# The second attention step with three score buffers, tiles prepared two ahead, and the unit matrix of R added as rows by GpSimd

## What is computed

```python
R = S + eye(N); R = R / R.sum(-1)            # S is adj here, N = 4096
Xf = Xa = X
for n in range(2):                           # two steps
    logits = (Xa @ W1.T @ W2.T) @ (Xa @ W3.T).T
    probs = softmax(logits)                  # 4096 x 4096
    A = the largest entries of each row up to a mass of 0.9, renormalised
    Xf = R @ Xf
    Xa = A @ Xa
    Z = Z + Xf @ U1[n].T + Xa @ U2[n].T
out = layernorm(X + Z) * ln_g + ln_b
```

## Time and profile before

| | |
|---|---|
| median of 3 runs | 4354.27 us (4349.45 to 4354.54) |
| the profiled execution | 4350.77 us |
| its span, first to last instruction | 4349.0 us |
| PE busy in the span | 3762.5 us (87%) |
| DVE busy | 3623.6 us (83%) |
| ACT busy | 3114.5 us (72%) |
| GpSimd busy | 1017.3 us (23%) |

### The profile page before, as it was taken

One profiled execution on the slowest core, in us unless ns is written; L12 is line 12 of the kernel. 1 busy time (PEld: TensorE's weight loads), 2 busy tenths in 40 slices (PEclk: granted clock), 3 DMA queues, 4 the chain that ended last, 5 costly groups with the idle time before them and its releaser, 6 DMA issues.

```text
span 4349.0 us, 66313 instructions
## 1 busy us (share of the span) xinstructions
PE 3762.5 (87%) x25364; PEld 3163.1 (73%) x25364; DVE 3623.6 (83%) x6400; ACT 3114.5 (72%) x3128; POOL 1017.3 (23%) x1412
## 2 busy tenths in 40 slices
PE   8677877777777769999999749999999999999996
PEld 5677777777777747777778547777777777778875
DVE  2899999999999939888888188888888889999995
ACT  3789889898989845555555367777777777777771
POOL 0000000000000000001010224444444445555555
PEclk9899999999999989999999979999999999999998
DMA  3211111111111020000000212222233423333332
GB/s 116 93 45 66 45 55 56 47 64 47 64 47 64 27 78 12 19 16 19 16 17 17 87 35 85 87 83 88 88 93 93 134 90 105 107 107 105 100 104 73
DMA packets 131759, 292.49 MB, mean 67 GB/s; under 512 B 14122, under 2 KB 94186, under 8 KB 127058
## 3 DMA queue, kind: packets, MB, share of 16 engines
q1 hardware_dynamic: 131410, 287.99, 20.6%
HBM read 250.19 MB, written 37.75 MB: 66 GB/s over the span
## 4 chain that ended last, share of the span: by engine, by line
PE 34%; ACT 28%; DVE 14%; issue 14%; POOL 10%; DMA 1%; DVEq 0%; SPq 0%; ACTq 0%; POOLq 0%
PE ps L803 11%; PE ps L642 9%; DVE b L1226 7%; ACT b L871 6%; ACT b L988 5%; ACT b L989 5%; DVE b L1173 3%; ACT b L865 3%; PE ps L792 3%; ACT b L971 3%; PE ps L748 3%; PE ps L623 2%; POOL b L468 2%; ACT b L859 1%; PE ps L780 1%
## 5 line engine op out<-in xcount | busy, mean ns | idle before, releaser
L707 PE MATMUL ps<-b 128*128 128x257 f32 x4096 | 902.1, 379 | 0.0
L803 PE MATMUL ps<-b 128*128 128x257 f32 x4096 | 900.9, 379 | 0.0
L642 PE MATMUL ps<-cb,b 128*128 128x128 f32 x4096 | 606.9, 312 | 321.7 <-ACT b L865 321.7
L707 PEld LDWEIGHTS ps<-b 128*128 128x128 f32 x4096 | 775.6, 189 | 118.3 <-issue 3.8
L803 PEld LDWEIGHTS ps<-b 128*128 128x128 f32 x4096 | 770.2, 189 | 111.7
L642 PEld LDWEIGHTS ps<-cb,b 128*128 128x128 f32 x4096 | 546.1, 163 | 371.1 <-ACT b L865 329.6
L1137 DVE SCALAR_TENSOR_TENSOR b<-b 128x4096 f32<-128x4096 f32 x128 | 566.4, 4425 | 63.1 <-ACT b L859 59.8
L1139 DVE CUSTOM_DVE_ANT_0 b<-b 128x4096 f32<-128x4096 f32 x128 | 566.3, 4425 | 5.5 <-DMA b<-in_adj 1.1
L871 ACT ACTIVATE b<-ps 128x1024 f32<-128x1024 f32 x512 | 499.9, 1023 | 75.6 <-PE ps L642 74.0
L623 PE MATMUL ps<-b 128*64 128x128 f32 x8192 | 504.0, 276 | 0.0
L865 ACT ACTIVATE b<-b 128x4096 f32<-128x4096 f32 x128 | 474.4, 3706 | 8.0 <-DVE b L1141 8.0
(11 more groups left out here) (186 smaller groups left out, 4743.2 us busy)
## 6 DMA issues: line engine op xcount, KB each, us to landing
b<-in_adjTb SPq DMA_DIRECT2D x256, 512.0 KB, 3.8
b<-in_adj SPq DMA_DIRECT2D x32, 2048.0 KB, 8.0
y_d<-b SPq DMA_DIRECT2D x64, 128.0 KB, 1.7
h_d<-b SPq DMA_DIRECT2D x64, 128.0 KB, 1.8
b<-h_d SPq DMA_DIRECT2D x64, 128.0 KB, 2.3
b<-in_xT SPq DMA_DIRECT2D x1, 4096.0 KB, 15.8
b<-in_x SPq DMA_DIRECT2D x32, 128.0 KB, 2.2
b<-y_d SPq DMA_DIRECT2D x32, 128.0 KB, 2.1
```

The source lines that it names most:

```text
L642: last = nc.tensor.transpose(bank(2 * (gq % 3), 2)[:, b * 128:(b + 1) * 128], ub[:, u % UB, j * 128:(j + 1) * 128], ident_s)
L707: last = mm(b[:, 0:XA], aj[:, q % AJR, e, :], xf[:, j, :], start=False, stop=(j == NT - 1))
L803: last = mm(o[:, 0:XA], at[:, q % ATR, b, :], xa[:, j, :], start=(j == 0), stop=(j == NT - 1))
```

## The change

In the second step there are three score buffers instead of two (`scores(s, t)` is `eb[:, t % 3]`, and the sums `zE` have three columns), and the tile that is prepared is two ahead: PE does `logits(n+2)` in iteration n, ACT copies it, exponentiates it only at the end of its iteration (`expo(n+2)` is the last call of `acts`), and GpSimd brackets it after `levels(n)`. `av_ev` and `mq_ev` move from ahead of the levels to behind level 1. DVE calls `rmax(t+2)` in `finish(t)`, between `mark` and the wait for the vote. Before the loop, tile 1's scores are made and exponentiated too. The first step keeps its order.

The unit matrix of R is no longer a product: `Rstart` only takes the PSUM bank, and `r_post` begins with one addition of 128 x 257 elements by GpSimd (`prs += xf[r]`).

To make room, AJR falls from 4 to 3, ACT's unused output `junk` is written as 8-bit floats instead of bf16, `gxs` shares `hin`, `u2` is loaded for one step at a time, `finx` has four buffers instead of six (SP waits for `f1` before it overwrites one), and the score buffers lose eight spare columns.

```diff
-    AJR = 4
+    AJR = 3
...
+        def scores(s, t):
+            return eb[:, t % (2 + s), 0:N]
...
+                    if m >= 2:
+                        sp.wait_ge(g["f1"], 2 * (m - 1))
...
                         po.wait_ge(g["rd"], r + 1)
+                        plink(tt(prs[:, i, :], prs[:, i, :], xf[:, r % NT, :], ALU.add))
...
                 if s == 1:
                     bracket(0)
+                    bracket(1)
...
                             r_post(p)
-                        if n + 1 < NT:
-                            bracket(n + 1)
...
                             levels(n)
+                        if n + 2 < NT:
+                            bracket(n + 2)
...
                 def Rstart(r):
-                    b = rslot()
-                    if r >= NT:
-                        pe.wait_ge(s_xl[r % NT // CT], 48)
-                    mm(b[:, 0:XA], ident_s, xf[:, r % NT, :], start=True, stop=False)
-                    return b
+                    return rslot()
...
-                    if n + 1 < NT:
-                        logits(n + 1)
+                    if n + 1 + s < NT:
+                        logits(n + 1 + s)
...
-                def acts(t, items):
+                def acts(t, items, n):
                     items = list(items)
                     for k in range(1, ACT_LEVELS + 1):
                         if t < NT:
                             level(t, k)
+                        if k == 1:
+                            if 1 <= n <= NT:
+                                av_ev(n - 1)
+                            if n >= 2 or n + 3 < NT:
+                                mq_ev(n - 2 if n >= 2 else None, n + 3 if n + 3 < NT else None)
                         if k >= ACT_LEVELS - 1 and items:
                             r_ev(items.pop(0))
                     for r in items:
                         r_ev(r)
+                    if n + 2 < NT:
+                        expo(n + 2)
...
                         for k in range(ACT_LEVELS + 1 if t else 1, r + 1):
-                            if k == r and t + 1 < NT:
-                                rmax(t + 1)
+                            if t == 0 and k == 3:
+                                rmax(1)
...
                     if s == 1:
                         mark(link, t, 0)
+                        if t + 2 < NT:
+                            rmax(t + 2)
```

More of the change, by code:

```diff
@@ L706, in Rpart @@
                             pe.wait_ge(s_xl[j // CT], 48)
-                        last = mm(b[:, 0:XA], aj[:, q % AJR, e, :], xf[:, j, :], start=False, stop=(j == NT - 1))
+                        last = mm(b[:, 0:XA], aj[:, q % AJR, e, :], xf[:, j, :], start=(j == 0), stop=(j == NT - 1))
                         if e == TBK - 1:
@@ L769, in mq @@
                         if tz is not None:
-                            last = mm(b[:, 0:256], xz[:, k, :], u2[:, s, k, :], start=(k == 0), stop=(k == 1))
+                            last = mm(b[:, 0:256], xz[:, k, :], u2[:, k, :], start=(k == 0), stop=(k == 1))
                     for k in range(2):
@@ L812, in _ @@
                 if s == 1:
+                    pe.wait_ge(s_l1, 16 * 10)
+                    mq(None, 2, zx(None, 2))
+                    logits(1)
                     Rmul(1)
@@ L1041, in _ @@
                 if s == 1:
+                    zx_ev(None, 2)
+                    mq_ev(None, 2)
+                    logit_ev(1)
+                    expo(1)
                     r_ev(1)
@@ L1057, in _ @@
                         zx_ev(tz, tx)
-                    if n + 1 < NT:
+                    if s == 0 and n + 1 < NT:
                         expo(n + 1)
-                    if 1 <= n <= NT:
-                        av_ev(n - 1)
-                    if zm:
-                        mq_ev(tz, tx)
-                    if s == 0 and tx is not None:
-                        gx_ev(tx)
-                    if s == 1:
-                        acts(n + 1, [2 * p + i for p in pairs_in(n) for i in range(2)])
+                    if s == 0:
+                        if 1 <= n <= NT:
+                            av_ev(n - 1)
+                        if zm:
+                            mq_ev(tz, tx)
+                        if tx is not None:
+                            gx_ev(tx)
+                    else:
+                        acts(n + 1, [2 * p + i for p in pairs_in(n) for i in range(2)], n)
                 barrier(ac, kS[s])
```

93 lines of the change are left out of this document (50 added, 43 removed).

## The result

The change makes the kernel slower: 4415.86 us in the median (4412.37 to 4417.04) against 4354.02 us (4349.45 to 4354.54) of the kernel before beside it, a ratio of 1.0143 with a 95% interval of 1.0125 to 1.0161. Forecast were 4374 us, between 4325 and 4400. The sign was right, the size was not.

The account below looks back on a forecast made before the run. It took PE's own round as the new bound, replacing a loop over four engines. Start +0.5, 28 rounds +26.6, ends -4.6, -5.2, -1.6, reload +7, on 4350.8, gave 4373.5, said as 4374 us, range 4325 to 4400.

Parts of the forecast that it names:

- T to E: Second step, end of second R product (T) to ACT's first `Tr` copy (E): 5.56 us each round, against 4.65 before.
- the stop behind the third chunk: PE's idle stretch after transposing three `Tr` chunks, waiting for a PSUM slot from ACT: 4.0 us each round.
- S to T: Start of `AV` (S) to the end of the next second R product: 43.2 us, from 44.08 less 0.88.
- the reload: Reload of xf at iteration 16, behind GpSimd's last R tiles: once +7 us, between 0 and 15.
- ring and 8-bit output: Three adj chunk buffers, if SP issues at once, and ACT's 8-bit `junk`: both to cost nothing on the path.
- E to S: ACT's first `Tr` copy to the start of `AV`: 8.5 us, depending on PE's clock, bounds 6.29 and 9.17.
- What is late next: PE's own round is late, `expo` standing before the first `Tr` copy: 57.3 us per round, +26.6 us over 28.
- The first rival: Clock holds or falls less behind PE's stop: 55.05 us per round and 4311 us if held; 4308 to 4345, chance 0.15.
- GpSimd drags SP: Rival: from iteration 17 late `r_post` delays SP's adj chunks, PE stops inside R products; +32, 4406 us, chance 0.12.
- It is still ready in time: DVE's mask, some 12 us early in the first half, about 10 us later in the second, never delays PE.
- The identity product: Removing R's identity products saves PE 0.88 us per round; GpSimd's addition, some 3 us per iteration, off the path.
- The third rival: PE goes free of ACT: T to E stays at its old mean of 4.65 us or shrinks; 4331 us, chance 0.10.

Follow-up runs that it names:

- the best version: Changed kernel with `expo` before the second R copy, `final_add` before the bracket, reload swap, one adj chunk before output stores, identity products back: 4251.21 us, ratio 0.977.

## Why the prediction was right or wrong

**What held.** The chain left DVE's search and went onto PE's round. `expo` starts 0.6 us after T, T to E is 5.53 to 5.55 us in nearly every round (5.56 said), the stop behind the third chunk 3.99 us (4.0 said), S to T 43.2 us. In the first half masks come some 12 us ahead of T, as said. The last iteration is 46.32 us (46.4 said), the reload +5.3 us over a round (+7 said), and ring and 8-bit output cost nothing: a pass of a level takes 3709 ns (L1000), as the 3.7 us of before.

**E to S, under "What is late next": mis-sized.** I took 8.5 us, from four rounds of before whose stop was like the new one. Over iterations 1 to 17 it is 153.92 / 17 = 9.05 us, with the clock at 0.63 in nearly all. One of the rounds and the sum, which answer to the earlier trace rows:

```profile
2786.24:2795.45 9.21, 8.14 (x28) 4.32 (x29) 8.99 (x9) 7.16 (x8) 8.93 (x7) 0.63 0.00 0
...
sum 153.92, PE 135.63 PEld 71.66 DVE 147.54 ACT 121.17 POOL 148.73; mean PE 7.98 PEld 4.22 DVE 8.68 ACT 7.13 POOL 8.75
```

The round settles at 58.00 us, and E to S then stays at 9.1 to 9.3 us, while before it went from 6.29 to 9.17. The four rounds of before with a like stop were no measure of it; even the upper bound of 9.17 was a little low. That the stop alone doesn't fix the price is shown by the run with the identity products: the same stop of 4.0 us, round after round, and 7.9 to 8.7 us behind it. In the first half the term comes to 14 x 0.55 = 7.7 of the 8.4 us. In the second E to S is 8.6 us in the mean, near the forecast. The first rival (the clock holds) is ruled out by the same rows, and its 55.05 us per round was right for the case in which it does hold: the run with eight filling products had 55.07.

**"GpSimd drags SP", the second rival: it was not an alternative but came on top.** I treated it as a case of 0.12 beside the forecast, though nothing in the forecast excluded it, and so the sum has nothing for PE's waits inside the R products. The step that failed is the position of `r_post`: I said the first chunk's issue at T + 34, from R tiles done by T + 28 or so. In the round shown they are done at T + 31.5, and the issue is at T + 38.2; over iterations 17 to 28 the R tiles are done between T + 27.6 and T + 31.5, and the issue is between T + 33.5 and T + 38.2. I had named one held instruction of the bracket, the row of 4.31 us. There are three in the round shown: two in the bracket (4.49 and 4.56 us) and one in `r_post` (4.73 us for the scaling), beside three passes of DVE. The need was nearly where I had it, T + 40.6 against T + 39.8. Here the rule that I called a smaller matter decides: the Trainium skill, SBUF — State Buffer, section Who interferes with whom, has such a GpSimd instruction wait while DVE's two-input pass holds the port. The rows fit it: the scaling takes 4.73 us beside L1255, a pass with two inputs, and ends with it, and 0.48 us one tile later beside L1261, which has one input. No run here took DVE's passes away. I had asked only whether DVE is held, not whether GpSimd is, and what waits behind it on SP's queue. The price of the lateness is paid twice here too. In the round shown above PE waits 1.95 us for the chunk, and then the other 80 instructions take 19.34 us; at the pace of the 48 ahead of the stop, 10.60 / 48 = 0.221 us each, they would take 17.7. The two make 3.6 us, and this round is 61.85 us where its neighbours without a stop have 57.9. Over 13 rounds it is 16.2 us of waits and 10.9 us of slower products, 27.1 of the 28.4 us. Iteration 30, which I had put at 52.1 us with no such stop at all, takes 61.54 us:

```profile
4264.25 15.95 PE L810 MATMUL ps<-b 128*128 128x257 f32 x64
...
4296.61 20.38 PE L714 MATMUL ps<-b 128*128 128x257 f32 x80 [5.11 <-DMA b<-in_adjTb]
```

It has the longest wait for a chunk, 5.11 us, and both `AV` (14.08 us at full clock) and the instructions behind the wait run at a low clock, 0.88 and 0.86 in the mean.

**"It is still ready in time", under "Three buffers, two tiles ahead": true, with nothing to spare.** From iteration 18 on the masks come between 3.5 us ahead of T and 0.5 us behind it, about the 12 less 10 us that I had said, and PE waits for them for 1.5 us in all, where I had said never. What I had not seen is where the 10 us come from: DVE waits for `final_add` for 62.5 us in 13 rounds, because that now stands behind the bracket. The run that moved only SP's loads gained about 10 us and then met the mask: 38.9 us of PE's waiting. So two things had almost no slack, and I had named only one of them as a rival.

**"The identity product": -0.88 us per round, forecast as a gain on the path, was none.** The run with the products put back had the same first half and, in its trace, a second half that was 11 us shorter. What I put "nothing on the path" for, GpSimd's addition, is on the path in the second half, by way of SP's queue. In the best version, where the two kernels ran side by side, the whole trade is 17 us the wrong way.

**The third rival** is ruled out, for the reason given: PE's slot is missing because ACT is late. I had weighed the Trainium skill, Perfetto Trace Analysis, section Optimization Strategy, by which a gap that repeats can mean too few buffers. The third score buffer left the stop and made it longer (3.99 us against 3.23 in the earlier trace rows); moving one call on ACT removed it. But with that call moved the change as a whole does pay, 51.6 us per round against 56.5 in the first half. How much of this is the buffer can't be said: it is what lets a tile be prepared two ahead, but no run separates it from the calls that moved with it.

What stays open: why the fall of the clock is smaller with the identity products in place (E to S 7.9 to 8.7 us against 9.2), and what the bracket's place alone costs. No run put `r_post` ahead of the bracket in more than one iteration, and none gave the changed kernel its fourth chunk buffer back.

## What to carry to other kernels

Before an engine's instruction is moved, ask what the instruction ahead of it waits for: work that needs no input from the bound engine belongs ahead of that wait, not behind it; here one call's place was worth 95 to 99 us. Then follow each in-order queue behind the moved step (here GpSimd's R tiles, then SP's chunks) in the half of the program in which it has the most to do, and add the rivals that can happen together. An instruction taken off the busiest engine has won nothing until the engine that gets it has been looked at for what waits behind it.

## What the chip showed that I had not expected

A stop of 4.0 us on PE cost 4.0 us and then 2.9 more: behind it the granted clock went down to its half level for part of the next stretch, 0.63 in the mean of 9.2 us, in round after round, and adding PE work to fill the stop made the kernel some 30 us faster. Short GpSimd instructions are not short when DVE runs a long pass with two inputs: 4.49 us for one column, 4.73 us for 128 x 256, against 0.48 us for the same scaling beside a pass with one input. And before GpSimd's reduction over the partitions, the vote of `levels` (L469), the engine stands idle for 82.1 / 13 = 6.3 us. The profile shows nothing that it waits for, but the idle time begins with two short instructions MODIFY_POOL_CONFIG in GpSimd's sequencer:

```profile
POOL b L469 <- issue: 82.1, 13, 7.5
```

```profile
L469 POOLq MODIFY_POOL_CONFIG  x26: 4/9/16, 3512.7 to 4237.3; - x26
L469 POOL PARTITION_ALL_REDUCE b<-b x13: 388/391/392, 3518.5 to 4243.0; - x13
```

Each vote has the same pair again behind it, ahead of GpSimd's next instruction. In the kernel before that is `final_add`, and there GpSimd stands idle once more, for 94.7 / 12 = 7.9 us. So the turn to the vote and back takes some 14 us of GpSimd's time in a round of about 56 there; that the configuration is the cause is argued from the order of these rows and was not tested.
